# Latent attention: row sums spread over all rows of a head, inverted per group of heads, and the causal mask added in VectorE's peak search

## What is computed

```python
kv_d = x @ kv_d_w
q_d = x @ q_d_w
k_p = (kv_d @ k_u_w).reshape(b, s, NH, RD)
q_p = (q_d @ q_u_w).reshape(b, s, NH, RD)
v = (kv_d @ v_u_w).reshape(b, s, NH, HD)
k_r = apply_rope((x @ rope_k_w).reshape(b, s, NH, RD), cos, sin)
q_r = apply_rope((q_d @ rope_q_w).reshape(b, s, NH, RD), cos, sin)
k = jnp.concatenate([k_p, k_r], axis=-1)
q = jnp.concatenate([q_p, q_r], axis=-1)
scores = jnp.einsum('bqhd,bkhd->bhqk', q, k) * scale
scores = jnp.where(causal[None, None], scores, jnp.finfo(scores.dtype).min)
probs = jax.nn.softmax(scores, axis=-1)
out = jnp.einsum('bhqk,bkhd->bqhd', probs, v).reshape(b, s, H)
return out @ o_w
```

## Time and profile before

| | us |
|---|---|
| median of three runs | 2232.35 |
| lowest and highest | 2229.02, 2239.0 |
| the profiled execution | 2229.9 |
| its span, first to last instruction | 2228.2 |
| latent attention in it, about | 1589 to 1904 |

### The profile page before, as it was taken

How to read it: one execution, slowest core, us unless ns; L and a number is a source line. 1 busy time by engine, 2 the same in 40 slices (tenths; PEclk the granted TensorE clock), 3 DMA queues, 4 the chain that set the end, 5 groups by cost and what they waited for, 6 DMA issues and landing times. The chain is left out here.

```text
span 2228.2 us, 43433 instructions
## 1 busy us (share of the span) xinstructions
PE 2151.3 (97%) x18048; PEld 1793.0 (80%) x18048; DVE 1315.5 (59%) x2315; ACT 1082.5 (49%) x1919; POOL 672.5 (30%) x684
## 2 busy tenths in 40 slices
PE   7999999899999999999999999999899998999996
PEld 5766776444589999999999999999777776899996
DVE  7676776689854445444544455454655455767773
ACT  5777533687743344333433343333455544325552
POOL 4111110466422121111111111211354644035663
PEclk9999999999999999999999999999999999999998
DMA  7445202100133223312312223221000000258995
GB/s 294 142 147 171 72 1 115 57 1 1 51 130 122 87 86 114 114 58 76 113 61 111 76 86 112 86 77 39 26 2 2 2 2 30 89 196 260 278 275 104
DMA packets 46931, 215.32 MB, mean 97 GB/s; under 512 B 6160, under 2 KB 6160, under 8 KB 32400
## 3 DMA queue, kind: packets, MB, share of 16 engines
q1 hardware_dynamic: 29968, 139.13, 17.2%
q0 software_dynamic: 16768, 73.41, 11.6%
HBM read 169.00 MB, written 43.52 MB: 95 GB/s over the span
## 5 line engine op out<-in xcount | busy, mean ns | idle before, releaser
L343 POOL TENSOR_TENSOR c_prob<-c_prob,c_inv_mass 128x512 f32<-128x512 f32 x128 | 130.4, 1038 | 353.2 <-DVE c_inv_mass L335 353.2
L325 ACT ACTIVATE c_prob<-abc_banks,c_neg_peak 128x256 f32<-128x256 f32 x256 | 117.7, 472 | 177.7 <-DVE c_neg_peak L317 177.6
L50 PE MATMUL abc_banks<-bc_xt,bc_wq_hi 128*128 128x256 f32 x512 | 147.7, 288 | 0.0
L50 PE MATMUL abc_banks<-c_ctx,c_wk_hi 128*128 128x256 f32 x512 | 146.6, 286 | 0.0
L51 PE MATMUL abc_banks<-bc_xt,bc_wq_hi 128*128 128x256 f32 x512 | 144.9, 283 | 0.0
L52 PE MATMUL abc_banks<-bc_xt,bc_wq_lo 128*128 128x256 f32 x512 | 144.8, 283 | 0.0
L51 PE MATMUL abc_banks<-c_ctx,c_wk_hi 128*128 128x256 f32 x512 | 143.7, 281 | 0.0
L52 PE MATMUL abc_banks<-c_ctx,c_wk_lo 128*128 128x256 f32 x512 | 143.7, 281 | 0.0
L238 PE MATMUL abc_banks<-ab_wq,b_xqt 128*128 128x512 bf16 x512 | 118.7, 383 | 4.3 <-DVE b_h L209 2.2
L2200 DVE TENSOR_TENSOR c_v_lo<-abc_banks,c_v_hi 128x512 fp32r<-128x512 f32 x64 | 44.3, 692 | 133.1 <-ACT c_v_hi L2116 133.1
L1936 POOL DMA_DIRECT2D c_ctx<-kept_scratch x24 | 13.2, 550 | 347.0 <-PE abc_banks L52 347.0
(11 more groups left out here) (594 smaller groups left out, 7211.3 us busy)
## 6 DMA issues: line engine op xcount, KB each, us to landing
bc_xt<-kept_scratch POOLq DMA_DIRECT2D x24, 1024.0 KB, 5.1
c_ctx<-kept_scratch POOLq DMA_DIRECT2D x24, 1024.0 KB, 5.2
e_raw<-e_w SPq DMA_DIRECT2D x15, 1536.0 KB
x_res<-b_w SPq DMA_DIRECT2D x34, 512.0 KB, 5.5
bc_raw<-c_w SPq DMA_DIRECT2D x16, 1024.0 KB, 4.9
h_res<-e_w SPq DMA_DIRECT2D x7, 1536.0 KB
kept_scratch<-bc_xt SPq DMA_DIRECT2D x8, 1024.0 KB, 3.9
kept_scratch<-c_ctx SPq DMA_DIRECT2D x8, 1024.0 KB, 3.9
```

The lines of the kernel that those rows point to most:

```text
L50: pe.matmul(out, lhs[0], rhs[1], start=first, stop=False)
L325: ins = act.activation(self.prob[:, u % 2, j, :], self.s_ps[:, j, :], ACT.Exp, bias=self.neg_peak[:, u % 2, j:j + 1], accum_out=self.mass[ ...
L343: pool.tensor_tensor(part, part, self.inv_mass[:, u % 2, js].unsqueeze(2).to_broadcast([P, 2, SEQ]), ALU.mult).then_inc(self.prob_done, 1)
```

## The change

It does four things, all in the latent attention.

1. The mask is no longer added by TensorE. `mask` is now f32 with 256 columns, zeros in the first 128 and the causal mask in the last 128. `find_peak` adds it and takes the maximum in one instruction, per head and query tile (eight instructions a group, four over 128 columns and four over 256); each writes the masked scores back to `s_ps` and one maximum per partition to `peak`. The peaks are no longer negated there; ScalarE negates them when it copies them.
2. `masses` multiplies with a matrix of ones of 32 columns, so that each row of a head gets the head's sum, and the two groups of a pair lie beside each other in the bank (256 columns each). The number of products and their size are as before.
3. `inverses` is gone, and with it the places n0 and n1 of the ring. `invert` and `divide` run per group, over 128x256; `divide` reads `inv_mass` from SBUF.
4. The order: the first group's sums of the first pair follow its weighing, and the second group's wait until the first have been inverted (they share a bank). On ScalarE `output_high` of the first pair moves behind the high parts of k. VectorE inverts and divides the first pair before the low parts of q. Of the second pair it inverts and divides the first group before search 0 and the second group between searches 0 and 1. In the last turn the second pair's groups have banks of their own (m1, z1).

Cut to its core:

```diff
         PLACES = (("lq", 1), ("lk", 1), ("mt", 0), ("q0", 1), ("q1", 1), ("k0", 1), ("k1", 1), ("m0", 0), ("v0", 1),
-                  ("qt0", 1), ("qt1", 1), ("n0", 0),
-                  ("kt0", 1), ("kt1", 1), ("m1", 0), ("xt0", 2), ("xt1", 2), ("n1", 0), ("v1", 1), ("o0", 0), ("o1", 0))
+                  ("qt0", 1), ("qt1", 1),
+                  ("kt0", 1), ("kt1", 1), ("m1", 0), ("z1", 0), ("xt0", 2), ("xt1", 2), ("v1", 1), ("o0", 0), ("o1", 0))
...
-            pool.memset(mask_f[:, :], 0.0).then_inc(blanked, 1)
-            pool.memset(neg_peak[:, :, :], 0.0).then_inc(blanked, 1)
-            pool.wait_ge(blanked, 2)
-            pool.affine_select(out=mask_f[:, :], in_=mask_f[:, :], compare_op=ALU.is_ge, fill=-1e30, base=0,
+            pool.memset(mask[:, :], 0.0).then_inc(blanked, 1)
+            pool.memset(peak[:, :, :], 0.0).then_inc(blanked, 1)
+            pool.memset(ones[:, :], 1.0).then_inc(blanked, 1)
+            pool.wait_ge(blanked, 3)
+            pool.affine_select(out=mask[:, P:], in_=mask[:, P:], compare_op=ALU.is_ge, fill=-1e30, base=0,
...
-                            pe.matmul(s_ps[:, j, cols], q[mine, c, tok], k[mine, c, :], start=n == 0, stop=n == 2)
-                for t in range(TB):
-                    for j in range(4):
-                        mm = pe.matmul(s_ps[:, j, 2 * t * P:(2 * t + 1) * P], ident_b[:, :], mask[:, :], start=False, stop=True,
-                                       skip_group_check=True)
+                            mm = pe.matmul(s_ps[:, j, cols], q[mine, c, tok], k[mine, c, :], start=n == 0, stop=n == 2)
...
-            def masses(i, h):
-
-                bank = claim(f"m{h}", i)
-                for r in range(2):
-                    n = C * i + 2 * h + r
-                    for t in range(TB):
-                        for j in range(4):
-                            mm = pe.matmul(bank[HD * j:HD * (j + 1), t * P:SEQ], share[:, r, :], prob[:, n % PROBS, j, t * SEQ:SEQ + t * P],
-                                           start=r == 0 and t == 0, stop=r == 1 and t == TB - 1)
-                mm.then_inc(ring_ready, 1)
-
-            def inverses(i, h):
-
-                await_free(pe, f"m{h}", i)
-                bank = claim(f"n{h}", i)
-                for r in range(2):
-                    mm = pe.matmul(bank[:, r * SEQ:(r + 1) * SEQ], spread_f[:, r, :], inv_mass[:, :], start=True, stop=True)
-                mm.then_inc(ring_ready, 1)
+            def masses(i, h, r, bank):
+
+                n = C * i + 2 * h + r
+                for t in range(TB):
+                    for j in range(4):
+                        mm = pe.matmul(bank[HD * j:HD * (j + 1), r * SEQ + t * P:(r + 1) * SEQ], ones[:, :],
+                                       prob[:, n % PROBS, j, t * SEQ:SEQ + t * P], start=t == 0, stop=t == TB - 1)
+                return mm
+
+            def first_masses(i, r):
+
+                if r == 0:
+                    pe.wait_ge(ring_free[use_of["m0", i] % BANKS], use_of["m0", i] // BANKS)
+                    masses(i, 0, 0, bank_of("m0", i)).then_inc(mass_half, 1)
+                else:
+                    pe.wait_ge(inverted, 2 * i + 1)
+                    masses(i, 0, 1, bank_of("m0", i)).then_inc(ring_ready, 1)
 
...
                 if now:
                     turned_scores(i, 1)
                     weigh(i, 0)
+                    first_masses(i, 0)
                 if nxt:
                     keys(i + 1, 1)
                 if now:
                     turned_scores(i, 2)
                     weigh(i, 1)
-                    masses(i, 0)
+                    first_masses(i, 1)
                 if nxt:
                     values(i + 1, 0)
                 if now:
                     turned_scores(i, 3)
                     weigh(i, 2)
+                if i == BATCH - 1:
+                    masses(i, 1, 0, claim("m1", i)).then_inc(ring_ready, 1)
                 if nxt:
                     turn_queries(i + 1, 0)
                     turn_queries(i + 1, 1)
-                if now:
-                    inverses(i, 0)
                 if nxt:
                     turn_keys(i + 1, 0)
                     turn_keys(i + 1, 1)
                 if now:
                     weigh(i, 3)
-                    masses(i, 1)
+                if now and nxt:
+                    bank = claim("m1", i)
+                    masses(i, 1, 0, bank)
+                    masses(i, 1, 1, bank).then_inc(ring_ready, 1)
+                if i == BATCH - 1:
+                    masses(i, 1, 1, claim("z1", i)).then_inc(ring_ready, 1)
                 if after and now:
                     turn_inputs(i + 2, 0)
                     turn_inputs(i + 2, 1)
                 if i == -1:
                     keep_busy(pe, s_ps[:, 0, :], parts["v_u"][0][:, 0:P], parts["v_u"][0], 5)
                 if nxt:
-                    if i == -1:
-                        pe.wait_ge(mask_done, 1)
                     scores(i + 1, 0)
                 if i == -1:
                     turn_inputs(1, 0)
                     turn_inputs(1, 1)
                     keep_busy(pe, o_ps[:, :, :].rearrange("p h q -> p (h q)"), parts["v_u"][0][:, 0:P], parts["v_u"][0], 3)
                 if now:
-                    inverses(i, 1)
...
-                act.activation(peak_t[:, :], bank_of("mt", i)[:, 0:SEQ], ACT.Copy).then_inc(free_of("mt", i), 1)
+                act.activation(peak_t[:, :], bank_of("mt", i)[:, 0:SEQ], ACT.Copy, scale=-1.0).then_inc(free_of("mt", i), 1)
...
-                await_free(act, f"n{h}", i)
+                act.wait_ge(divided, 2 * (2 * i + h) + 2)
...
-                if now:
-                    output_high(i, 0)
                 if nxt:
                     for t in range(TB):
                         turned_high("kt", i + 1, t, kt_hi, kt_hi_done)
+                if now:
+                    output_high(i, 0)
                 if now:
                     output_raw(i, 1)
...
             def find_peak(s, c):
-                dve.wait_ge(s_ready, C * s + c + 1)
                 if s > 0:
                     await_ready(dve, "mt", s - 1)
-                dve.tensor_reduce(neg_peak[:, 0, c::HD], s_ps[:, :, 0:P], AX.X, ALU.max, negate=True)
-                dve.tensor_reduce(neg_peak[:, 1, c::HD], s_ps[:, :, P:P + SEQ], AX.X, ALU.max, negate=True).then_inc(peak_done, 1)
-
-            def invert(i, h):
-                await_ready(dve, f"m{h}", i)
-                if 2 * i + h > 0:
-                    await_ready(dve, f"n{1 - h}", i - 1 + h)
-                dve.reciprocal(inv_mass[:, :], bank_of(f"m{h}", i)[:, 0:SEQ]).then_inc(free_of(f"m{h}", i), 1)
-
-            def divide(i, h):
-                await_ready(dve, f"n{h}", i)
-                dve.wait_ge(o_raw_done, 2 * i + h + 1)
-                dve.tensor_tensor(o_f[:, :, :], o_f[:, :, :], bank_of(f"n{h}", i).rearrange("p (r q) -> p r q", r=2),
-                                  ALU.mult).then_inc(free_of(f"n{h}", i), 1)
+                dve.wait_ge(s_ready, C * s + c + 1)
+                for t in range(TB):
+                    cols = slice(t * P, P + t * SEQ)
+                    for j in range(4):
+                        ins = dve.tensor_tensor_reduce(s_ps[:, j, cols], s_ps[:, j, cols], mask[:, P - t * P:], 1.0, -3e38, ALU.add,
+                                                       ALU.max, peak[:, t, c + j * HD:c + j * HD + 1])
+                ins.then_inc(peak_done, 1)
+
+            def last_pair(i, h):
+                return i == BATCH - 1 and h == 1
+
+            def invert(i, h, r):
+
+                n = 2 * i + h
+                name = "z1" if last_pair(i, h) and r == 1 else f"m{h}"
+                if h == 0 and r == 0:
+                    dve.wait_ge(mass_half, i + 1)
+                else:
+                    await_ready(dve, name, i)
+                if n > 0:
+                    dve.wait_ge(divided, 2 * (n - 1) + r + 1)
+                done = free_of(name, i) if r == 1 or last_pair(i, h) else inverted
+                dve.reciprocal(inv_mass[:, r, :], bank_of(name, i)[:, r * SEQ:(r + 1) * SEQ]).then_inc(done, 1)
+
+            def divide(i, h, r):
+                n = 2 * i + h
+                if r == 1 or last_pair(i, h):
+                    await_free(dve, "z1" if last_pair(i, h) and r == 1 else f"m{h}", i)
+                else:
+                    dve.wait_ge(inverted, n + 1)
+                dve.wait_ge(o_raw_done, n + 1)
+                dve.tensor_tensor(o_f[:, r, :], o_f[:, r, :], inv_mass[:, r, :], ALU.mult).then_inc(divided, 1)
...
                 if now:
-                    invert(i, 0)
+                    invert(i, 0, 0)
+                    invert(i, 0, 1)
+                    divide(i, 0, 0)
+                    divide(i, 0, 1)
                 if nxt:
                     for t in range(TB):
                         low("qt", i + 1, t, qt_lo, qt_hi, qt_hi_done)
-                if now:
-                    divide(i, 0)
                 if i == BATCH - 1:
```

(22 more changed lines are left out.)

4 lines of the change are left out of this document (2 added, 2 removed).

## The result

The changed kernel took 2234.78 us, median of 20 runs (2231.87 to 2243.83), and the kernel before 2229.34 beside it (20 runs, 2228.38 to 2239.16): a ratio of 1.0018, 95% interval 1.0010 to 1.0026. By the ratio the change costs 4.0 us (2.2 to 5.8), and the two medians lie 5.4 us apart; I had forecast 13. The profiled execution has a span of 2234.6 us against 2228.2.

The account below looks back on a forecast made before the run. TensorE bounds the kernel before; after the change VectorE was to bound each turn. Turn -1 1.8, turns 0 to 5 8.1 and turn 6 2.4 sum to 12.3, with the memset 13 us: 2232 + 13 = 2245 us, range 2227 to 2275.

Parts of the forecast that it names:

- K: Time of one masked peak search on VectorE, eight instructions with accumulator reads: 2.88 us, from 1.83.
- rival 1: VectorE's accumulator read costs nothing or is absent: search about 2.2 to 2.5 us, kernel time 2228 to 2234 us; chance 0.17.
- Rival 2: VectorE's search instructions and reads don't overlap: search 3.4 to 4.2 us, kernel time 2264 to 2286 us; chance 0.23.
- (a) to (c): TensorE's savings a turn: mask products 1.7 us, second spreading products 0.73, earlier second half of k 0.6; up to 3.1.
- (a): TensorE's mask products go, eight per group of heads in four groups: 1.7 us a turn saved.
- (c): Without the first spreading products, TensorE's turning of k starts its second half 0.6 us earlier, limited by a bank.
- The first pair's inverses are free: VectorE's two inverses for the first pair fit in its 9.77 us hole and before q's low parts: no cost.
- The queue of the second pair: VectorE's work from the second pair's first inverse to the last peak: 18.3 us, making a turn 1.35 us longer.
- Turns 0 to 5: Six latent attention turns, each 1.35 us longer with VectorE as the bound: 8.1 us in all.
- Turn -1: Three steps between scores and to the peaks, where VectorE decides, grow from 3.45 to 4.05 us each: +1.8 us.
- Turn 6: The turn without latents for a later sequence goes from 36.14 to 38.6 us, VectorE as bound: +2.4 us.
- chain that stays as long: Turn 7, which searches nothing: its last outputs wait for a chain of unchanged length, so ±0.5 us.

Follow-up runs that it names:

- the hybrid: Kernel before without mask in the search, the first pair's sums in all rows and inverted in pieces as in the changed kernel: 2213.13 us, ratio 0.9919.
- the longer search: Changed kernel with one more VectorE instruction (a maximum over the mask's 256 columns) at the head of every search: 2248.55 us, ratio 1.0089.

## Why the prediction was wrong

The sign of the change was right: it costs time. The size was not, 4 to 5.4 us for 13. And the sign was right in part by luck: the steady turns and turn 0, which carried 8.1 of the 13 us, cost nothing, and the loss stands in the first turn and the last two.

- **The step that failed** is the term K = 4 x (0.21 + 0.34) + 8 x 0.085 = 2.88. The main instructions were priced rightly: the one step without a read is 0.21. The read was taken as the smallest VectorE instruction, 0.085 us beyond its overlap. It is 0.14 us long but adds 0.04 to a step: the steps are 0.25 and 0.38 us. A search takes 2.49 us, and with it went the mechanism of the forecast, a turn that VectorE bounds from end to end. From K = 2.54 down, as rival 1 says, the turn is the old one or less. That the read is an instruction of its own, as the profile shows, does not shut rival 1 out, as the prediction had it: a read that costs next to nothing is its first half. Rival 2 is out: each search instruction starts 0.08 us or more before the one ahead has ended.
- **The base.** 2245 stands on 2232.35, the median of three runs; 20 runs of the kernel before give 2229.34. Of the 10 us between 2245 and 2234.78 the base is 3. Rival 1's 2228 to 2234 us stand on the same base; counted from 2229.34, the measured time lies 3 to 4 us above them.
- **Two sums don't follow from their terms.** Rival 1 has -4 to +2 us; its turns of 36.5 to 37.1 give -4.8 to -1.2 in turns 0 to 5 and +0.4 to +1.0 in turn 6 (36.14 before), and with its -0.5 for turn -1 that is -4.9 to -0.7. And 12.3 us became 13 "with the memset", which was priced at ±0.2.
- **TensorE's savings** (a) to (c) were right in sum, 3.1 against 3.2 us measured in the busy time of a steady turn. (a) is 1.5 to 1.6 rather than 1.7 (37.29 against 35.83 without masks), (c) 0.68 rather than 0.6 (the hybrid).
- **The first pair's inverses are free**: shown by the hybrid, which also shows that turning k waits for the bank as forecast.
- **The queue of the second pair**, 6.8 + 4K, and the waits of TensorE: right in structure. At K = 2.81 the longer search gave 38.38 against 38.3. At 2.49 the queue and TensorE's work are about level, which fits that taking work from either alone, in the last part of the turn, gained little. My forecast of 1.9 and 1.8 us of waiting became 1.36 and 1.34; rival 1 had 1.2 and 1.2.
- **Turns 0 to 5**: 8.1 us forecast, -0.2 measured. The error in K is 6 x 4 x 0.39 = 9.4 here, more than the whole term.
- **Turn -1**: 1.8 forecast, 1.97 measured, for other reasons. From the first scores to the peaks there are four steps. The three in which VectorE decides (the first, the second and the last) were to grow by 0.6 each; they grew by 0.37, 0.27 and 0.27, 0.9 in all. The other 1.06 us is in the third step, from 1606.4 to 1612.5, where TensorE follows a wait of 1.85 us: the granted clock is 0.50 to 0.55 until 1610 and 1.00 behind it, and the window from 1606.40 on has 0.83, where the kernel before has 1.00. Every run whose searches 0 and 1 are masked has this low clock, and none with plain maxima alone; with all four masked it is 17.4 us or more from the first scores to the peaks, 15.43 before.
- **Turn 6**: 2.4 forecast, 2.93 in the first profile and 1.80 in the second. Held at full clock the turn took 37.1, so +0.9 by K, the rest the half clock.
- **Turn 7**: ±0.5 forecast, +1.15 and +0.12 in two profiles. Here the profile of the kernel before misleads: it has a low clock of its own (0.50 and 0.65 from 1894 to 1898 us, behind a wait of 2.35). Three kernels with the second pair as before took 28.24 to 28.30 at a clock of 1.00, five with it in pieces 29.10 to 29.18 (the other four profiles are 0.5 to 1.6 us longer; in the first one the last outputs ran at a clock of 0.62). So the pieces cost 0.9 us, and the "chain that stays as long" was a second error. From the start of the last pair's inverse to the end of its division VectorE takes 4.54 us, and 3.66 with the spreading products. The changed kernel's rows:

```profile
1896.15 1.75 DVE L2994 RECIPROCAL d_inv_mass<-d_ring 128x256 f32<-128x256 f32 x1
1898.14 0.43 DVE L3003 TENSOR_TENSOR d_o_f<-d_o_f,d_inv_mass 128x256 f32<-128x256 f32 x1 [0.25 <-ACT d_o_f L2857]
1898.49 1.75 DVE L2994 RECIPROCAL d_inv_mass<-d_ring 128x256 f32<-128x256 f32 x1
1900.27 0.42 DVE L3003 TENSOR_TENSOR d_o_f<-d_o_f,d_inv_mass 128x256 f32<-128x256 f32 x1
```

  In the run with only the masked search one inverse starts at 1890.74 us, VectorE waits 1.22 us for the spreading products, and the whole division, 0.69 us from 1893.71, ends it.

So errors partly cancelled. By the prediction's own rate, 3.1 us for every 0.1 of K, the searches were priced 12 us too high. Left out were the low clock, 0.8 to 2.0 us in turn 6 and part of the 1.06 in turn -1, which I had nowhere priced as something that new waits may cost, and 0.9 us in turn 7.

The chances leaned on slower by over 0.5%; measured is 0.2%, inside the band of no change that can be told, and inside the range.

## What to carry to other kernels

Price a change by the stretch between the last input and the first thing that waits for it, not by an engine's idle share: here VectorE had 18 us a turn to spare and the same two inverses were worth 0.68 us of gain in its hole and 0.35 us of loss in the serial stretch. Two edits that each lean on the same slack have to be costed together; each alone won 0.6 to 0.7 us a turn, both together 0.1. Where the steady turns come out level, the first and the last ones decide: here they hold all of the loss.

And ask of each computation that is moved whether it is needed at all. The shift of a softmax need not know the mask when the masked terms are zeroed afterwards; leaving it out, with the cheap half of the change, gave 0.9919 where the change gave 1.0018. This has a limit that no run here tries: where a masked score lies far above all scores that count, the shift makes every exponential that counts vanish, and the division by their sum fails.

## What the runs showed of the hardware

- VectorE's read of the accumulator is an instruction of its own of 0.14 us, but it runs beside the next main instruction and adds 0.04 to its step (0.21 us without a read, 0.25 with one, for 128 columns).
- Writing 256 columns to PSUM in place while reading them showed no cost of its own: a step of 0.38 us, of which 0.04 is the read's. The rest, 0.34, is what an addition from PSUM of 0.42 us gives less an overlap of 0.08.
- A VectorE pass with two operands in SBUF doubled GpSimd's products beside it, 0.91 for 0.45 us, and itself went from 1.41 to 2.10 for two. VectorE's idle time is not free where GpSimd's queue is on somebody's path.
- The granted clock does not follow from these waits alone. Waits of 1.36 and 1.34 us a turn left it at its upper level in all steady turns of both profiles. With 1.68 us twice it fell in two of five steady turns, for 1.29 us each. With waits of 2.4 and 0.6 us in turn 6 it was 0.50 over 5.9 us in one profile and 0.76 over 7 us in the next. Behind a wait of 2.35 us in turn 7 it fell in the kernel before and not in the run with only the masked search.
